# The orders in which five engines take their steps, laid anew for a two-layer decoder block in one program

## The reference

```
x = x + L0_attn(layernorm(x));  x = x + L0_xattn(layernorm(x), ctx);  x = x + L0_ffn(layernorm(x))
x = x + L1_attn(layernorm(x));  x = x + L1_xattn(layernorm(x), ctx, itok);  x = x + L1_ffn(layernorm(x))
```

## Time and profile before

| what | value |
|---|---|
| median of three runs | 2307.28 us (2307.23 to 2309.33) |
| the profiled execution, its span | 2313.3 us |
| TensorE busy | 1964.8 us (85%) |
| VectorE busy | 1603.6 us (69%) |
| ScalarE busy | 1255.5 us (54%) |
| GpSimd busy | 1124.5 us (49%) |
| mean granted clock of TensorE | 0.931 |
| DMA | 147.35 MB |

### The profile page before, as it was taken

One profiled execution on the slowest core, in us unless ns is written; L12 is line 12 of the kernel. 1 busy time (PEld: TensorE's weight loads), 2 busy tenths in 40 slices (PEclk: granted clock), 3 DMA queues, 4 the chain that ended last, 5 costly groups with the idle time before them and its releaser, 6 DMA issues.

```text
span 2313.3 us, 66487 instructions
## 1 busy us (share of the span) xinstructions
PE 1964.8 (85%) x27020; PEld 1633.0 (71%) x27020; DVE 1603.6 (69%) x4253; ACT 1255.5 (54%) x2880; POOL 1124.5 (49%) x1336
## 2 busy tenths in 40 slices
PE   5899978889788998899999689667588999898982
PEld 3767757677576776777777478667477888697882
DVE  6589786787857888678767835665889666854232
ACT  5457875467654777657765435234344455443551
POOL 2775336742367633675255354351877222234466
PEclk8999989999899999999999789789699999998996
DMA  4000000000000000000010065797011000026994
GB/s 142 5 6 2 2 1 6 6 2 2 1 3 6 3 2 1 5 5 3 2 38 13 8 187 167 222 235 266 25 28 31 4 9 9 4 83 228 349 315 125
DMA packets 98047, 147.35 MB, mean 64 GB/s; under 512 B 32016, under 2 KB 72464, under 8 KB 97488
## 3 DMA queue, kind: packets, MB, share of 16 engines
q1 hardware_dynamic: 88656, 124.48, 17.0%
q0 software_dynamic: 9088, 18.63, 3.3%
HBM read 126.49 MB, written 16.58 MB: 62 GB/s over the span
## 4 chain that ended last, share of the span: by engine, by line
PE 53%; DVE 24%; issue 8%; POOL 8%; ACT 4%; DMA 2%; SPq 0%; POOLq 0%; DVEq 0%; ACTq 0%
PE PS L2108 5%; PE PS L2092 5%; PE PS L1578 3%; PE PS L1584 3%; PE PS L1060 3%; PE PS L674 3%; PE PS L660 2%; POOL GOT L1736 2%; DVE mx L1054 2%; DVE P L1056 2%; PE PS L1067 2%; PE PS L1075 2%; PE PS L1036 2%; DVE zo L636 2%; PE PS L1171 2%
## 5 line engine op out<-in xcount | busy, mean ns | idle before, releaser
L2122 ACT ACTIVATE wh<-PS,we 128x128 f32<-128x128 f32 x624 | 176.0, 373 | 231.5 <-PE PS L2092 231.0
L1990 POOL DMA_INDIRECT wx<-x,INV x156 | 153.1, 981 | 204.5 <-PE PS L2099 106.0
L2092 PE MATMUL PS<-wxT,we 128*128 128x128 f32 x1248 | 176.3, 289 | 42.5 <-issue 35.1
L1054 DVE TENSOR_REDUCE mx<-PS 128x8 f32<-128x512 f32 x256 | 176.1, 688 | 45.8 <-PE PS L1049 24.0
L640 POOL TENSOR_TENSOR xrs<-xrs,Cs 128x2 f32<-128x2 f32 x112 | 82.0, 732 | 255.0 <-DVE xrs L632 252.7
L2108 PE MATMUL PS<-we,wh 128*128 128x128 f32 x1248 | 181.4, 290 | 22.8 <-DVE wxT L2140 21.1
L2092 PEld LDWEIGHTS PS<-wxT,we 128*128 128x128 f32 x1248 | 161.0, 202 | 49.5 <-issue 48.7
L2108 PEld LDWEIGHTS PS<-we,wh 128*128 128x128 f32 x1248 | 163.8, 202 | 32.2 <-DVE wxT L2140 29.3
L1056 DVE TENSOR_TENSOR P<-PS,mx 128x512 f32<-128x512 f32 x256 | 177.1, 692 | 8.9
L1060 PE MATMUL PS<-Cs,P 128*128 128x128 f32 x1024 | 157.5, 287 | 28.1 <-ACT P L1473 21.0
L1500 POOL TENSOR_TENSOR km<-qk,Cs 128x1024 f32<-128x1024 f32 x64 | 121.1, 1898 | 119.8 <-ACT qk L1458 48.1
(11 more groups left out here) (359 smaller groups left out, 5427.2 us busy)
## 6 DMA issues: line engine op xcount, KB each, us to landing
we<-in_wf SPq DMA_DIRECT2D x78, 578.0 KB, 5.6
we<-in_wl SPq DMA_DIRECT2D x78, 578.0 KB, 5.9
yf<-wy SPq DMA_DIRECT2D x78, 64.0 KB, 5.1
ys<-wy SPq DMA_DIRECT2D x78, 64.0 KB, 5.1
x<-X SPq DMA_DIRECT2D x32, 128.0 KB, 1.9
R<-in_wa SPq DMA_DIRECT2D x1, 3072.0 KB, 14.6
wx<-x,INV POOLq DMA_INDIRECT x156, 5.5
X<-in_x SPq DMA_DIRECT2D x4, 512.0 KB, 15.0
```

Of the source, the lines that this page charges most:

```text
L1054: e.tensor_reduce(A.mx[r], S3, AX, ALU.max).then_inc(*o.inc())
L1990: e.indirect_dma_start(out=WB[s].x[q // NS % NX], out_offset=None, in_=x1[k], in_offset=bass.IndirectOffsetOnAxis(ap=INV[k % NH][:, q - T0 ...
L2092: i = e.matmul(ps(s, 1)[:, 128 * f:128 * f + 128], w[:, 128 * f:128 * f + 128], B.xT, True, True)
L2122: i = e.activation(B.h[:, 128 * f:128 * f + 128], ps(s, 1)[:, 128 * f:128 * f + 128], ACT.Relu, bias=w[:, 512 + f:513 + f])
```

## The change

Only the strings of `ORDER` differ: for phase "one" those of TensorE (pe), ScalarE (act), VectorE (dve) and GpSimd (pool), for phase "last" those and SP's (sp). Each string has the same length and the same number of each character. No step program, wait or buffer differs. The diff, cut to the strings of which the text speaks:

```diff
 ORDER = {
     "one": {
         "pe":
-            "311002230010112223033013002003120000011011022122010201211021332031302102102012013213120102001320313123232321231031113032002320322131301300100120032031"
-            "233112311021001010222022112312132013310322022012013233133121032030312022100310033001303203210012101310120130122322313202112102130130202132200123201012"
...
+            "000011101122222033333013002031200000011012011220102201211013031032010220133021212132102120013233113223232321310001303220200331113130130100010222320130"
+            "121321121000011202201221123332312013310322022012132331331200320303112012003130300013022303210012013102131010122322312201121023301212320123001232100010"
...
         "dve":
-            "233200110100213122000313011000203330022302130111202103332200110221011120221120313221203333120012001032300001321003110221302230111120131122221010030223"
-            "120330213211210003133301322200231112132030301013222211331221330002230230211101133003132202032321100323331100220011220033313132211311000022000030220322"
...
+            "000111033312223200001101100022033330223130023301201122210001021101132202211113010222233330121002100233300001300211323110022301111223011120100222120321"
+            "203320133211120031010233322200331111023230313012222113321233000022303201111011330031322220023321100323310120200112023333311322111300200020000302232111"
...
     "last": {
         "pe":
-            "013123120013230113132003101212002113011300223100321102212203330211013221001123303120011213230223213110330100212221333310100212232311233102000303001011"
-            "120213320030112300102000231123221332011231232222222322232223323333332323333222322222232223232333333302323322322222201022222321313321233333232222222032"
-            "231222233333131003303333330022101122222223323222203333013311232333130111101231113111232102031300111132211123301230223300000000310001111112000010211110"
...
+            "113310022013231013130203101212020130211132030010231120122233020131013210201123303120121132300321223103300011212221333310112023312213322001000003001311"
+            "102231230030110231200100023213130222122113332222222233333222332233222333223332222233233332222333322230233222332320332212302212233222211332232022222332"
+            "221333123031123033302220330022121322113223332232111330321133332230313320021133131111321202031130011132211233102302211000100100103330020011010011021110"
...
         "dve":
-            "441051533022113300112200311322100033112230021122001313121200313112102033211210030223210331230003121362266666666666666660630112233300111230230011622233"
-            "312121322323323223233021022211332132120302113300321010232223003331102210331002210331223302002313100221233102031310022036610310666661666610666660016606"
-            "660601610316031060321621306321036201362130262310631062106320236231060163162031232001201331230120222000111333445444050055145114004442522100515535220331"
-            "100005201254355500324201111404212205140252305345504000444520315320000333100323515545241502144402125552224204032222532002444513111555432013200340101113"
-            "443113342205034014104233443325313051552220223300001103300001210102112332333231321222212122223221131111223010311112213002122223211002311323300032001121"
-            "112331313233022222123312222022001033220331231230313300011011221000032220301226613666666666663662003266623601023133312130023333000332001122223031102203"
-            "311011101133333133010100003010633123232212111132322133311321236612666606166660666620336101232103301100103313221100310330132202031130036320022303230032"
-            "02331011033232311113332010022020123324024410211055512202304134420103551544343115351351041324435155344455544455544455545",
+            "111133330000112222001323203111120001012222001333311212031311120003220213320032211132013331130266666666166600066606633322223001111230326161623122223332"
+            "232332112323320003203212132231121203102302311001032312331000222120333312023003120122302103301310222032013313010236016106666606066616661600616066660601"
+            "613301630106031226231063102363012623021612036310620331220610613206032132301022161303602101322013444445550000554441111400422205552110051533322203100100"
+            "555025124443335004201111022221055520530434440500042255503211533000015033244441235554120051042122224442040533555222213250141134443221003200341011135413"
+            "332200555044403111304333230512212202333000010303000112201112322332533311212222121222221331131112223001301111223100222223211140112233003300203121111213"
+            "333320022222112033301222221033022023121333321300001011121000033222213266063666666663226600023662630602311133321360323330000301112222233003101033210111"
+            "101333011333106000103361033122232123211321121233331321132662160026016331600120316610123036016363201032163103021601323032106306636023103200232032330103"
+            "20213130203211321133012002031223144420025553121010233244400115551234443113555310344413055513213444555444555444555444555",
         "pool":
-            "376495012802311301323020211101103002223233111111000212231031132002230323233220300311110777788889989899896968668099181010111177000227323020300736762623"
-            "276332622233633779666677797886697999688978968879867986444455554444450045554014154512200101411552552325022355454304540035555543335441114424224555555544"
-            "440445400550053335550450404444400555522254544422445455215115254222050404114434433151411144435553322233330000011103332222222112102200011122211113303001"
-            "113332223333222222233300011100222000001133331300101113233331113330788899666888899777681837897676868979676977696969977668888969689679897799867648444554"
-            "4559554474474455555544444455554554444455555544444455554455445555444444555555444544455555",
+            "331100221303120211100010222233331111110002223311100322102333222333200030111166999778888978689800099978688760911191118770002222333007032262633367222333"
+            "766679976679869968789667877978778969666988874444455555444445000455005111445451122200415522553332555244000455335551445543411142225544555554434400044554"
+            "500055333550044554445454022255445444055222445111225244550005411144333424115544333133222335100000011100333222222221112111004211222110003331113333322233"
+            "222222333200011122200000011103333331100013322233111133300086887877788668699111989333776968869678967698669789876977966988897996679768768444445554575574"
+            "4444984555957955444444555555444444555555444444555555444444555555444444555555444444555555",
         "sp":
-            "64589a02137baaaaaaaab2233262637372626372626372367621137376aa6771515001504a150415aaa04888a81504a4015041532320b51404bb8804158015488370418532678401573882"
-            "604237615880413578204632670145731526042601435775646457aaaaaaaaaaaa22a00262626aa1162a332651045126047351405104373762154051370432676240513704730426376204"
-            "73402653711540736237155137042604621537269042651041956240739615473991753193754596759799999999",
+            "aaaaaaaaa2223332662377636237622732632676113627713667557171500015a0104455414010bb880158a4a580324a81aa4a5a0421045b3b0848b8510184083175530421783760868482"
+            "314278560853064212803714655347720126013675456475464572aaaaaaaaaa0a02226a6a2a6a12613a236150125406130457175346023410431757062374207314032640543672037571"
+            "46032473561572301476515062342061234056461275071205317543147371355766994457695799999999999999",
```

More of the change, by code:

```diff
@@ new lines @@
+            "232221331331300003022020311131010010010322203203121121102110010202223330223121311231031020220211233231310032303203201121000013030132203032113000120310"
+            "110121303030212212112101233232001311300012230332323201123030231112133331232312210022202200303203002030003300113330130223110102313110102212111202201203"
+            "323121213312321000120230033202312213003010303032032032311131300311001003222323210210112010133313123232232121002110213013333032232232010210033133213232"
+            "002303110313022021002103323111023121103221212332332331013113221221323323103132121032332311220033",
@@ new lines @@
+        "act":
+            "000111012220023332133001000320032013312121021203111220120231013330021020132010120131223212131000302220030301111310301122203013012302120120012102112122"
+            "333123120323022033121331320023030011230031031010300311220020112023112012322311122012021332023213300121300003323202113030223001111130222323320321122321"
+            "133001201033211133333012232033303123010332013201301231121003022113132200003300222031110310110330310102221201022133301021232213132121033231322332123100"
+            "103323323200231101303011220020012120012102211233003001332011323113231322023231201013323320021130001110130122330110222001211033202333300230103113122333"
+            "012023012220120013332130021132101020322231132133000022200301110310011003322201132101022011120222013331223112331202020323123131003320230020110010331103"
```

(9 more changed lines are left out.)

75 lines of the change are left out of this document (29 added, 46 removed).

## The result

The kernel after takes 2354.51 us in the median of four runs (2346.73 to 2360.97), the kernel before 2308.31 beside it (2307.23 to 2314.15): a ratio of 1.0181, with a 95% interval of 1.0156 to 1.0205. On a second chip it was 1.0155 (1.0134 to 1.0177). The change makes the kernel slower by 46 us on the first chip and 35 on the second; I had said 12 faster.

A forecast was written before the change was run, and what follows sets the result against it. TensorE was taken to lead, with other limits (VectorE, DMA, GpSimd) in some stages. The terms -10 - 2 - 3 + 0 + 2 + 1 + 0 gave -12 us, 2295 as a median; range for 8 in 10, 2268 to 2318.

The forecast's parts named there:

- The first 1260 us: First phase and first attention of the last: sign open, taken as 0, bounds 22 us either way.
- T: The experiments' theory: in the first phase's new strings, a slot's successive TensorE steps stand too close, awaiting another engine's round trip.
- The bound of 22: First 1260 us: all 22.2 us of TensorE's waits for VectorE's normalizing step go, or the same comes on top.
- Slower, the rival at 0.26 (2318): First phase: VectorE's queue puts statistics and normalization behind other slots' work, 1.9 us each; 2318 us, chance 0.26.
- The clock: Rival, 60 to 1260 us: closing gaps raises TensorE's granted clock and removes idle time; 2270 us, chance 0.18.
- what would show it: Signs of a wrong forecast: first phase's end over 5 us off, or clock from 60 to 1260 differing by over 0.01.
- Dense experts: 1640 to 2090 us: TensorE's waits for VectorE's accumulations (L1634) shrink by 5.65 and 4 us; together -10.
- First routing: 1260 to 1330 us: TensorE's 16.28 us wait ends some 7 us sooner, but VectorE is the bound; -2.
- First mixture's tiles: 1460 to 1640 us: SP issues tile 40's weight load earlier, so TensorE's 14.93 us wait moves later; -3.
- Turnaround: The 22.61 us TensorE wait: GpSimd's sequence is the same, VectorE swaps two neighbours; 0.
- Last gathers: GpSimd's chain that ends the kernel gets three more tile fetches inside it, +3.7 us at most; taken as +2.
- Table loads: ScalarE: 92 function-table loads instead of 91, at 1.28 us for one beside TensorE; +1, bounds 0 and +1.3.

The follow-up runs named there:

- e1: The kernel before with after's four strings of the first phase; the last phase is before's. Ratio to before 1.0149.
- e5: e1 run once more, as reference for later kernels: before with after's four first-phase strings. Ratio to before 1.0159.
- e11: e5 with small moves in all four strings of the first phase at once. Ratio to before 0.9986.
- e6: e5 with 93 of the 1296 steps in TensorE's first-phase string moved by one to nine places. Ratio to before 1.0069.
- e12: Before with small moves in its own four first-phase strings, and after's last-phase strings only from 1640 us of before's trace on. Ratio to before 0.9951.
- e7: e5 with 80 of the 1280 steps in VectorE's first-phase string moved by one to nine places. Ratio to before 1.0111.
- e9: The kernel before, unchanged, run and profiled again; its profile is as the first one to 5 us.
- e10: The kernel after, unchanged, run and profiled again on a chip of the first kind. Ratio to before 1.0155.
- e13: Before with after's last-phase strings only up to the end of the first mixture's sparse tiles, before's from there on. Ratio to before 1.0056.
- e2: Before with after's five strings of the last phase; the first phase is before's. Ratio to before 1.0036.
- e16: The same kernel as e12, run once more on a chip of the second kind. Ratio to before 0.9962.

## Why the prediction was wrong

*The first 1260 us, taken as 0 with +-22: the step that failed.* It is +39, measured by itself as +35 to +38 (e1, e5) and taken back by e11. The prediction had one count that pointed there, "the queue that ends the wait loses work worth 7 us ahead of it and gets work worth 37 us", and set it against nothing. The other, "TensorE's string now changes slots more often (2062 to 2302 changes over both phases)" pointed nowhere for this stage: all of the rise is in phase "last" (1063 to 1314), while in the first phase, where the time is lost, the changes fall from 998 to 987. More steps of one slot stand directly behind each other there, which is what T says. I looked only at the waits that before had, and asked whether the new order shortens them; the cost lies at pairs of steps that had no wait before and so had no row. The measure that would have shown it needs only the old trace: for each step of TensorE, the work that its string puts between it and the slot's previous step, against the time that the slot's round trip took in the old trace (its lower quartile, by kind of step). In the first phase the pairs that are too short rise from 234 to 292, and the missing time from 145 to 181 us: 35 us more, beside 25.5 us of new idle time. For the last phase, where the dense experts won, it falls from 260 to 202. The measure gives a sign for this pair of strings and no price. In a count of the same kind (its kinds of step are drawn a little otherwise, so before has 149 us and after 184) e6's string still misses 175 us, though it won 22 on the chip, and e12's 157, though that kernel beats before.

*The bound of 22.* It came from the largest kind of wait. With many short new waits no row of before bounds the sum; and the row had the normalizing step under one of its names only (the waits for zo; those for x from the same line add 10.1 us from 60 to 1260).

*Slower, the rival at 0.26 (2318).* The side was right, the mechanism only in part. It named VectorE's queue; e7 puts 12 of the 38 us there, e6 22 with TensorE's. And the sum of VectorE's waits fell (84.3 to 79.0). Its time was too low as well, 2318 for 2354.5.

*The clock.* The rival had it as a gain, and its sum was off: a third of 121 us is 40, not 15, so as described it came to 2245 and not 2270. It went the other way: up to 13.8 us of the 39.4. Of the two signs under "what would show it" the first came, an end of the first phase over 5 us off; the clock from 60 to 1260 us fell by 0.01 (0.97 to 0.96), which is not more than the 0.01 named. By the Trainium skill ("TensorE: Matmul & The Clock Gate", section "What's actually happening") idleness throttles the array and activity releases it; the trace agrees, as the clock rose from 0.95 to 0.96 where e6 took 15 us of idle time away. The total of idle time alone doesn't set TensorE's busy time, though: e11 has 139.9 us idle, less than any profile of before's first phase, and 1043.7 busy, more than all six of them. Why is open.

*Dense experts, -10 (bounds -14 and +5): right in sign and in the wait named.* Measured -12 between e9 and e10 and between e9 and e12, -17 in the first pair, outside the bound. The wait for L1634 fell by 11.5 us, as the terms 5.65 + 4 said, but TensorE's idle time by only 6.0 (8.2 between e9 and e10); the rest, 10.9 us (4.8), is shorter busy time at a higher clock, which the term did not have. That the number came near is in part luck.

*First routing, -2 (bounds -7 and +2): not told from nothing,* +2 or -3, as the stage is counted from the first phase's last step or from r_count. The 16.28 us wait is gone (the longest two near it are 4.43 and 3.61), and as I said it bought little, since VectorE is the bound.

*First mixture's tiles, -3 (bounds -15 and +4): wrong sign,* +7 to +8, on the other chips +13 with the first routing (e13). The wait vanished, the stage is not shorter: the stage moves the same bytes at 240 for 248 GB/s. My reason, that the stage is full of DMA anyway, was right and should have put the gain at 0; the rest was not foreseen.

*Turnaround, 0 (bounds -1 and +1):* 23.90 for 22.61 us, just outside. *Last gathers, +2:* the 64 take 91.3 us from the first to the last issue (90.9 before): +0.5. *Table loads, +1:* 92 for 91, as counted; what the one load more cost can't be seen in the total. Each lasts 1283 ns, and ScalarE's next instruction starts 11 to 12 ns behind nearly all of them in both traces (all but six of 181, which wait), so the drain that the prediction quoted is not there, and the row was the right price.

```profile
L1235 ACT ACT_TABLE_LOAD x20 | 25.7, 1283 | 0.4
...
L820 ACT ACT_TABLE_LOAD x1 | 1.3, 1283 | 0.0
```

## What to carry to other kernels

Where several slots share in-order queues, an order is judged by the pairs it makes, not by the waits it removes: for every step, is there as much other work between it and its slot's previous step as the round trip through the other engine lasts? The engine that a wait names need not be the one whose order is at fault; here ScalarE was named in most new waits, had been idle before it in nearly half of them, and its own string was worth 4 of 38 us, TensorE's 22. And idle time of TensorE can cost more than itself: 25.5 us of it came with 13.8 us more busy time at a lower clock; but e11 got the idle time back and hardly any of the busy time (0.9 us).

## What was not expected of the hardware

The same kernel takes 3% longer on some chips (2382 for 2308 us), and none of that is in the first phase: the same last phase takes 67 us longer in e5 than in e9, with a clock of 0.91 for 0.95 in the dense experts and 232 for 260 GB/s in the second mixture. Whether a change of order has another sign on another chip is not settled by these runs: e2 was +8.6 us, where the first chip's profile of after promised -9 for the same strings, but e2's kernel was not timed on a chip of the first kind; e12 and e16, one kernel on either kind, agree (0.9951 and 0.9962).

A semaphore's way between engines is short and regular in the traces of before and after (medians of 34 to 56 ns between ScalarE, VectorE and TensorE, about 80 ns from VectorE or ScalarE to GpSimd; only from TensorE to GpSimd it is longer, mostly 113 to 273), so a round trip of 1 to 2 us is almost all the other engine's instruction, and an order can be laid against it.
